# Storing the split q and k of attention layers 0 and 1 by partition halves instead of column halves

## The reference

```
x = x + tanh(g_xattn[i]) * attention_i(layernorm(x), ctx)
x = x + tanh(g_ffn[i])   * ffn_i(layernorm(x))
```

```
layer 0:  q = Wq x + bq,  k = Wk c + bk,  v = Wv c + bv     (16 heads of 8 channels)
layer 1:  q = x, k = v = c                                    (8 heads of 16 channels)
scores = q^T k * scale;  p = softmax(scores);  out = p v      (256 x 256 scores per head)
```

## Time and profile before

| what | us |
|---|---|
| median of three runs | 1250.78 |
| lowest, highest run | 1244.24, 1250.89 |
| time of the profiled execution | 1240.12 |
| span of the profiled execution (first to last instruction) | 1238.3 |
| TensorE busy (matmul) | 960.1 |
| VectorE busy | 655.5 |
| ScalarE busy | 438.1 |
| GpSimd busy | 388.8 |

### The profile page before, as it was taken

The page is one execution under the profiler, slowest core; times in us unless marked ns, Lnnn a source line. Parts: engine busy times, 40 slices in busy tenths (PEclk is TensorE's granted clock), DMA queues, the critical chain, the costliest instruction groups (busy, mean ns, idle before and its releaser), DMA issues.

```text
span 1238.3 us, 18952 instructions
## 1 busy us (share of the span) xinstructions
PE 960.1 (78%) x6616; PEld 565.7 (46%) x6616; DVE 655.5 (53%) x1548; ACT 438.1 (35%) x721; POOL 388.8 (31%) x527
## 2 busy tenths in 40 slices
PE   4899975885288799577648953898989999279993
PEld 1455544775044345456425741243434444246562
DVE  5778734342567513278662436978778781311111
ACT  1466651110044421155311420075646667012220
POOL 5223202122854000334213015165555656200002
PEclk9999996888578899899768985599999999689997
DMA  6344514654433000544233833101030000810002
GB/s 179 113 120 152 179 48 162 204 189 153 111 97 103 22 26 0 161 95 93 62 147 108 254 120 89 39 2 39 3 135 9 1 3 6 321 48 22 17 14 77
DMA packets 117437, 115.29 MB, mean 93 GB/s; under 512 B 71752, under 2 KB 107144, under 8 KB 114312
## 3 DMA queue, kind: packets, MB, share of 16 engines
q1 hardware_dynamic: 106496, 95.58, 25.0%
q10 hardware_dynamic: 7776, 10.10, 2.6%
q0 software_dynamic: 3072, 8.39, 2.2%
HBM read 88.17 MB, written 29.62 MB: 95 GB/s over the span
## 4 chain that ended last, share of the span: by engine, by line
PE 47%; DVE 15%; issue 7%; DMA 5%; POOL 5%; ACT 2%; SPq 2%; another core or an unknown queue 1%; POOLq 0%; DVEq 0%; ACTq 0%
PE psT L1123 7%; PE psT L1422 6%; PE psT L1274 5%; DVE mxp L1813 4%; PE psB L1238 4%; PE psB L1123 3%; PE psB L1436 3%; PE psO L1318 3%; PE psB L1487 2%; PE psT L1385 2%; PE psB L1463 2%; PE psO L1308 2%; PE psO L1306 2%; DVE mxp L1817 1%; SPq L2259 1%
## 5 line engine op out<-in xcount | busy, mean ns | idle before, releaser
L1813 DVE TENSOR_REDUCE mxp<-psB 128x1 f32<-128x512 f32 x256 | 163.0, 684 | 38.5 <-PE psB L1238 37.3
L1274 PE MATMUL psT<-whole 99*128 99x256 bf16 (+2 forms) x1024 | 156.2, 279 | 14.6 <-issue 8.2
L1817 DVE TENSOR_REDUCE mxp<-psB 128x2 f32<-128x512 f32 x192 | 122.1, 684 | 34.5 <-PE psB L1244 34.0
L1573 ACT ACTIVATE Pt<-psT,ln 128x1024 f32<-128x1024 f32 x96 | 106.4, 1113 | 63.7 <-PE psT L1274 62.8
L1274 PEld LDWEIGHTS psT<-whole 99*128 99x128 bf16 (+2 forms) x1024 | 96.8, 102 | 63.8 <-issue 32.1
L1573 ACT ACTIVATE Pt<-psT 128x1024 f32<-128x1024 f32 x96 | 98.1, 1024 | 59.3 <-PE psT L1274 57.3
L1244 PE MATMUL psB<-whole 96*128 96x256 bf16 x384 | 77.8, 315 | 52.4 <-issue 46.7
L1238 PE MATMUL psB<-whole 96*128 96x512 bf16 x256 | 97.3, 429 | 26.1 <-DMA whole<-scr_q 13.8
L2144 POOL TENSOR_TENSOR rstd<-vare,cst 128x1 f32<-128x1 f32 x64 | 35.8, 580 | 260.2 <-DVE vare L1731 260.0
L1422 PE MATMUL psT<-whole,qf 128*128 x176 | 80.7, 602 | 0.6 <-ACT qf L1622 0.6
L2201 POOL TENSOR_SCALAR nb_t<-Pt 128x1024 f16<-128x1024 f32 x64 | 66.8, 1044 | 37.4 <-ACT Pt L1573 35.3
(11 more groups left out here) (308 smaller groups left out, 1764.5 us busy)
## 6 DMA issues: line engine op xcount, KB each, us to landing
whole<-in_w SPq DMA_DIRECT2D x32, 512.0 KB, 4.7
whole<-in_w SPq DMA_DIRECT2D x5, 3072.0 KB, 10.3
xn<-scr_sorted ACTq DMA_DIRECT2D x42, 128.0 KB, 2.2
scr_q<-sq SPq DMA_DIRECT2D x48, 96.0 KB, 1.9
scr_k<-sk SPq DMA_DIRECT2D x48, 96.0 KB, 1.9
whole<-scr_k SPq DMA_DIRECT2D x24, 192.0 KB, 3.4
whole<-scr_k SPq DMA_DIRECT2D x72, 64.0 KB, 3.5
whole<-scr_q SPq DMA_DIRECT2D x64, 64.0 KB
```

The costliest lines, as they stand in the source:

```text
L1274: ins = pe.matmul(psT[:, s.n % 2, i * A.T:(i + 1) * A.T], lhsT=k_at[:, h * kw + s.c * P:h * kw + (s.c + 1) * P], rhs=q_at[:, h * A.T:(h + ...
L1573: act.activation(p_slot(A, s.p)[:, 0:4 * A.T], psT[:, s.n % 2, 0:4 * A.T], ACT.Exp, bias=bias).then_inc(T_used[s.n % 2], 1)
L1813: dve.tensor_reduce(mxp[:, s.un.g % 2, at:at + 1], psB[:, s.n % BANKS, :], AX.X, ALU.max).then_inc(bank_used[s.n % BANKS], 1)
L1817: dve.tensor_reduce(mxp[:, s.un.g % 2, at:at + 2], psB[:, s.n % BANKS, :].rearrange("p (h n) -> p h n", h=2), AX.X, ALU.max).then_inc(bank ...
```

## The change

In layers 0 and 1 (A.halves == 1) the two DMAs of a store no longer split the columns but the partitions: the first takes partitions 0 to 63, the second 64 to 127, each with the three parts and all 256 columns. The number of DMAs, their bytes (96 KB each), their order, their semaphores and counts and the place of all other instructions stay. A contiguous run is 256 columns of bf16, 512 bytes, instead of 128 columns, 256 bytes; there are 192 runs in a DMA instead of 384. For A.halves == 2 the same slices are written as before.

```
 def store(dst, src, sem):
     for m in range(2):
-        rows_ = slice(m * P, (m + 1) * P) if A.halves == 2 else slice(0, P)
-        at = 0 if A.halves == 2 else m * w
-        sp.dma_start(dst[:, rows_, at:at + w].rearrange("c p n -> p c n"),
-                     src[:, :, m * w:(m + 1) * w]).then_inc(sem, 16)
+        if A.halves == 2:
+            half, at = dst[:, m * P:(m + 1) * P, 0:w], src[:, :, m * w:(m + 1) * w]
+        else:
+            half, at = dst[:, m * 64:(m + 1) * 64, 0:2 * w], src[m * 64:(m + 1) * 64, :, 0:2 * w]
+        sp.dma_start(half.rearrange("c p n -> p c n"), at).then_inc(sem, 16)
```

## The result

The changed kernel is slower. Its seven runs have a median of 1253.9 us (1250.89 to 1258.16), seven of the kernel before beside them 1249.14 (1242.97 to 1250.89); the ratio is 1.0058, with a 95% interval of 1.0029 to 1.0086, or +7.2 us (+3.6 to +10.7). The forecast was 1249.5 and no change. The profiled execution took 1252.79 us, with a span of 1251.0. Two kernels of the experiments had one execution each of over 1360 us (layer 0 alone, and one DMA for each store the first time); these two are in no median or ratio.

The account below looks back on a forecast made before the run. Layer 1 was taken as bound by SyncE's issuing. Issue 0, layer 1 landing 0 and layer 0 landing summed to -0.1 us, giving 1240.0 profiled; the median's 10.7 us offset gave 1250.7, less 1.2 for scatter 1249.5, range 1241 to 1254.5.

Parts of the forecast that it names:

- What bounds layer 1: Layer 1: SyncE's issuing time sets the pace, 11.51 us a unit, and TensorE waits for it; not bytes, packets or arithmetic.
- Issue time of a store: SyncE's 26 store issues in layer 1's chain: no difference, 0 us, with bounds of -3.6 and +3.4 us.
- layer 3's row: Layer 3's stores, 512-byte runs on 128 partitions, issue in 0.360 and 0.490 us; taken as the new stores' issue time.
- a sign of being wrong: The forecast is wrong if the median issue time of L1043 moves by more than 0.1 us.
- the rival of a dearer issue: SyncE's queue in layer 1: 64-partition issues cost more, +2.6 us, +3.4 at the dearest, giving 1252 to 1254; chance 0.10.
- Landing of a store: Layer 1's stores land 0.1 us earlier, 1.9 instead of 2.0 us; 2.2 or more would show half the partitions slower.
- In layer 1, nobody: Layer 1: no instruction waits for a store's landing, as SyncE is busy until the gathers; 0 us.
- The term for the engines: DMA engines, layers 0 and 1: 0.37 us of moving per store instead of 0.46, 6 us given back over 64 stores.
- Who waits in layer 0: Layer 0: stores lie beside work that fills the stage; 0 to -0.1 us in each of three tight places.
- the rival of a clock that shifts in layer 1: TensorE in layer 1: a small shift changes its granted clock, 4 to 6 us at stake either way; chance 0.16.
- The bound of what can be told: Whole kernel: what can be told from no change is about 0.5%, 6.25 us.
- The 1.2 us taken off: Whole kernel: 1250.7 lowered to 1249.5, since earlier runs made a median below the upper pair likelier.

Follow-up runs that it names:

- layer 0 alone: Partition halves in layer 0 only, column halves in layer 1, against the kernel before: 1249.34 us against 1246.05, ratio 1.0024 (0.9995 to 1.0052).
- one DMA for each store: Kernel before with one DMA and a plain semaphore increment per q and k store, layers 0 and 1: 1239.27 us against 1246.05; again 1239.43 against 1248.43.
- extra issue: Kernel before plus one unrelated 16 KB DMA behind the k stores of each layer 1 unit: 1251.71 us against 1246.29, ratio 1.0025.
- layer 1 alone: Partition halves in layer 1 only, column halves in layer 0, against the kernel before: 1249.63 us against 1246.05, ratio 1.0026 (1.0001 to 1.0051).
- kernel of the shapes: Kernel before with layer 0's q and k stores cut differently by unit; two issues took 1.36 us for partition halves, 1.34 even and odd, 0.81 for 96 and 32.
- second probes: Kernel before plus 12 more shapes of small store, each issued twice while SyncE is idle; 120 partitions took 0.64 us an issue.
- two kernels with probes: Kernel before plus small stores issued twice each after layer 0's attention, 15 kinds, then 12; in the first, 64 partitions took 0.58 to 0.62 us an issue.
- first three units alone: Partition halves only in units 0 to 2 of layer 0, against the kernel before: 1248.67 us against 1248.43, ratio 0.9999 (0.9976 to 1.0022).
- 96 + 32: Kernel before with layers 0 and 1 storing by partitions 96 and 32, 512-byte runs: 1246.07 us against 1246.29, ratio 0.9984 (0.9962 to 1.0006).
- last five units: Partition halves only in units 3 to 7 of layer 0, against the kernel before: 1246.90 us, ratio 0.9994 (0.9974 to 1.0014).

## Why the prediction was wrong, step by step

*What bounds layer 1*: right. The prediction named SyncE's issue queue as the pace of layer 1, and the extra issue, layer 1 alone and the single DMA all move it: +0.5 us a unit in two of them, and 0.65 us less in the third (units 2 to 7), of the 1.0 us that its stores save, where a new wait begins.

*Issue time of a store*: this step failed, as the term "I take no difference". It was to be 0.49 us by layer 3's row and is 0.61 and 0.59. Layer 3's stores share the run length, the axes and the pitch, and differ in the count on the partition axis, which the prediction mentioned and passed over. The shapes show that just this count makes the price. The median moved by over 0.1 us, which the prediction had named as a sign of being wrong. The sum with the measured term is 26 x 0.12 = +3.1 us, near the 3.4 by which the stretch grew; the rival of a dearer issue, which was given a chance of 0.10, had the place and, with 2.6 to 3.4 us, the price. That the stated range, 1241 to 1254.5, holds the 1253.9 is no merit of the mechanism: its top is the highest run before plus the dearest issue.

*Landing of a store*: wrong in sign. 1.9 us was expected and 2.2 measured in layer 1. A later start of the data covers it, and the landing counts from the start of the issue: in unit 0 the first issue takes 0.71 us instead of 0.39, and the first data moves between 15.10 and 15.20 us instead of between 14.60 and 14.70, from issues at 13.77 and 13.75. The prediction took 2.2 us or more as a sign that half the partitions are slower; that is only a small part of it, as the next windows show. "In layer 1, nobody" waits was nearly right: SyncE now waits there once for a q store, in unit 1, for 0.2 us.

The term for the engines failed too. The stores were to take 31 ns of an engine per run, by layer 3's row, and 0.37 us each instead of 0.46. The q stores of unit 5 of layer 0 can be read by themselves, and move the same 196 KB in each of these windows: the kernel before, layer 0 alone with its lower and upper halves, and the kernel of the shapes with its even and odd halves.

```profile
97.20:100.00 2.80, 2.79 (x30) 1.52 (x30) 2.18 (x4) 1.61 (x3) 2.35 (x6) 1.00 0.31 70
101.30:104.10 2.80, 2.80 (x30) 1.49 (x30) 2.18 (x4) 1.60 (x3) 2.35 (x6) 1.00 0.31 70
98.80:101.60 2.80, 2.80 (x30) 1.50 (x30) 2.18 (x4) 1.61 (x3) 2.35 (x6) 1.00 0.24 70
```

The DMA share (0.31, 0.31, 0.24) times 2.80 x 16 gives 13.9 us of the engines for 768 runs before, 13.9 for 384 runs from lower and upper halves (36 ns each) and 10.8 for 384 from even and odd ones (28 ns). So in these windows nothing of the relief that was to add up to 6 us is left, and dividing by lower and upper partitions is what took it. The port rule of the Trainium skill ("SBUF — State Buffer", the section on the DMA port swizzle) says that partitions 0 to 63 reach half of the ports; even and odd partitions reach all of them by its table, and the difference between the two agrees with it in direction. In the landing it is worth 192 x 8 / 16 = 0.1 us, the 0.1 by which even and odd halves land earlier. In layer 1 only the one wait of 0.2 us could feel it.

*Who waits in layer 0*: wrong. "TensorE is busy for 140 of 156 us" was read as cover for the whole stage. The wait stood in the trace of before, before unit 2's first matmul of the maxima; after the change it is longer, and the matmul comes 1.3 us later.

```profile
54.14 0.38 PE L1244 MATMUL psB<-whole 96*128 96x256 bf16 x2 [2.28 <-issue]
```

```profile
55.41 0.38 PE L1245 MATMUL psB<-whole 96*128 96x256 bf16 x2 [2.83 <-issue]
```

The longer wait by itself is no sign of the change: with layer 0 as before it was 2.93 us in the kernel with layer 1 alone and 3.08 in the one with the second probes. The time of that matmul is a better one. Counted from unit 0's first q store it is 41.3 to 43.0 us in the four profiles with units 0 to 2 changed, and 39.5 to 40.9 in the six that store these units as before. Two parts of it come out the same in each of these ten traces. The stores of unit 0 push its gathers 0.75 us back, and those of unit 2 push theirs 0.45 us back (from the q store to the gather 3.3 instead of 2.5 us, and 4.8 instead of 4.3). In unit 1 the bulk loads (20.41 to 21.17 us) are issued ahead of the q store, and its gather comes at 29.83 instead of 28.84; but SyncE's wait for that store, 1.2 us before and 1.7 after, lies anywhere from 0.5 to 2.2 us in kernels with these units unchanged, so that this delay is passed on is not shown.

```profile
17.04 2.10 SPq L2260 DMA_DIRECT2D whole<-scr_q  x3
...
21.17 0.45 SPq L1073 DMA_DIRECT2D x<-in_x  x1
...
29.83 2.03 SPq L2260 DMA_DIRECT2D whole<-scr_q  x3
```

What it costs in the end is not settled. All of the change is 7.1 us in two comparisons, layer 1 alone 3.3, layer 0 alone 3.0 with an interval from -0.6 to 6.5, and its first three units alone nothing measurable. The profiles show layer 0 longer with the first units changed (121.9, 123.8, 125.7, 122.7 us from first to last q store) than without (119.5, 120.5, 118.0, 120.0 and, in the two kernels with probes, 121.2 and 122.9), but the sets overlap. In the profile after, layer 1 even begins at 314.50 us, only 0.2 later than before, though layer 0's last q store comes 2.5 us later.

*The clock*: the rival of a clock that shifts in layer 1 is not needed. SyncE's issues fill the stretch almost without a gap, and their own times give the 3.1 us. The granted clock from 314 to 432 us was 0.70 to 0.73 in the three profiles with layer 1's stores changed and 0.73 to 0.80 in the others; no run held it apart.

*The bound of what can be told*: the change was 0.58% and just above 0.5%, so layer 1's +3.4 us would have been "same" by the prediction's own terms; with layer 0's part it is not. *The 1.2 us taken off* because of the scatter of the executions had no ground in the change.

## What to carry to other kernels

A queue that only issues DMAs can be the bound of a stage, and then a DMA's price is its issue time, not its bytes: look for a timeline of issues without gaps and a compute engine that starts a fixed time behind it. The issue time of a new shape isn't to be taken from a row that differs in one axis; if there is no row with the same counts, the range has to hold the dearest row of that queue, and the cheaper way is to issue fewer DMAs (here one for two). A mean busy share doesn't say that a stage has no wait: look at the first units one by one.

## What the runs showed of the hardware

The issue time is not monotone in the number of partitions: 0.57 to 0.70 us at 64, lower, upper, from 32 on (0.62) or every second one, 0.64 at 120, and 0.36 to 0.50 at 48, 56, 60, 72, 80, 112 and 128, with no dependence on one or three runs at 64. The issue behind a dear one may be dear too (0.58 to 0.61 at 32, 80 and 128), and while transfers pile up 128 cost 0.61 to 0.62. Single issues of any shape took up to 1.9 us.

At 512 bytes a run took an engine 36 ns from the lower or upper 64 partitions, and 28 ns from every second one or, in the kernel with one DMA, from all 128 (share 0.24 in the same window). A 256-byte run from all 128 took 18 ns.

TensorE's clock in layer 0 went with the wait before unit 2, but loosely. Where the wait was 2.7 to 2.9 us (the changed kernel in both its profiles, either layer alone, the first three units) the granted clock of the stretch from 46 to 66 us was 0.91, the worth of some 3.5 us at 1.2 GHz, behind the wait. Where it was 2.0 to 2.3 us the clock stayed at 1.00 in four kernels (before, extra issue, 96 + 32, last five units) and fell to 0.91 in the two profiles of the single DMA; with 2.3, 2.4 and 3.1 us it fell to 0.83 in the kernels of the shapes and of the first and second probes. The window after the change, and the same with 1.00 before:

```profile
46.00:66.00 20.00, 16.83 (x150) 9.22 (x146) 12.99 (x31) 10.57 (x17) 4.89 (x11) 0.91 0.39 113
```

```profile
46.00:66.00 20.00, 17.39 (x166) 9.71 (x164) 14.75 (x35) 12.05 (x18) 5.33 (x10) 1.00 0.44 124
```

In it TensorE and VectorE were busy for 0.6 and 1.8 us less than before (busy columns 1 and 3), and TensorE did 150 matmuls instead of 166, a part of it because unit 2 starts later. A fall of the clock is a plausible part of layer 0's loss, and of the scatter between executions, but no run held the clock apart from the wait.
